# A selective-scan stage with a mixture of experts beside it: a ring of eight hidden units, second matmuls six units behind, the last gating and the expert choice moved to later steps

## The reference, cut to what matters

```python
# the scan, for 256 channels and 16 states (log/exp form in chunks of 32 tokens)
dA  = jnp.minimum(jnp.exp(delta[..., None] * A[None, None]), 1.0)
dBu = delta[..., None] * Bm[:, :, None, :] * u[..., None]
states = cum_dA * (h[:, None] + jnp.cumsum(dBuk * inv, axis=1))
yk = (states * Ck[:, :, None, :]).sum(-1)
# the experts: 1 shared + 8, hidden size 512; the best two of 8 by gate_logits
shared = jnp.einsum('th,hd->td', jax.nn.silu(x_flat @ shared_w1.T), shared_w2.T)
top_k_gates, top_k_idx = jax.lax.top_k(x_flat @ gate_w.T, 2)   # then a softmax over the two
h = jnp.einsum('td,ehd->teh', x_flat, experts_w1)
expert_out = jnp.einsum('teh,edh->ted', jax.nn.silu(h), experts_w2)
selected = jnp.einsum('ted,te->td', expert_out, gates)         # every expert for every token
```

## Time and profile before

| | us |
|---|---|
| median of 3 runs | 1534.01 (1529.97 to 1536.33) |
| the profiled execution | 1531.76 |
| its span, first to last instruction | 1530.0 |
| scan steps 0 to 63 | 52.13 to 554.84 |
| TensorE busy | 1300.1 (85%) |
| VectorE busy | 1209.3 (79%) |
| ScalarE busy | 1058.9 (69%) |
| GpSimd busy | 670.4 (44%) |

### The profile page before, as it was taken

One profiled execution on the slowest core, in us unless ns is written; L12 is line 12 of the kernel. 1 busy time (PEld: TensorE's weight loads), 2 busy tenths in 40 slices (PEclk: granted clock), 3 DMA queues, 4 the chain that ended last, 5 costly groups with the idle time before them and its releaser, 6 DMA issues.

```text
span 1530.0 us, 22554 instructions
## 1 busy us (share of the span) xinstructions
PE 1300.1 (85%) x8408; PEld 504.1 (33%) x8408; DVE 1209.3 (79%) x1443; ACT 1058.9 (69%) x1839; POOL 670.4 (44%) x650
## 2 busy tenths in 40 slices
PE   4364779888976988886499999999999998999998
PEld 1111234333443443332122222222222222236963
DVE  0799988898989871765699999999999997933522
ACT  3552388668836835453179998999899986997643
POOL 0688878967978856661403112111111123111430
PEclk9675689989988998997689999999999998999999
DMA  7222222212322302421212101100010000010210
GB/s 219 66 84 69 75 85 83 89 57 83 96 69 80 88 21 55 88 48 31 43 33 50 30 30 48 23 2 2 2 23 2 2 2 19 5 30 12 74 32 28
DMA packets 63696, 75.71 MB, mean 49 GB/s; under 512 B 8633, under 2 KB 39226, under 8 KB 63458
## 3 DMA queue, kind: packets, MB, share of 16 engines
q1 hardware_dynamic: 62818, 72.70, 17.5%
q0 software_dynamic: 768, 1.57, 0.3%
HBM read 66.04 MB, written 8.21 MB: 49 GB/s over the span
## 4 chain that ended last, share of the span: by engine, by line
PE 48%; DVE 27%; issue 10%; POOL 7%; ACT 6%; DMA 1%; SPq 1%; another core or an unknown queue 0%; DVEq 0%; POOLq 0%; ACTq 0%
DVE mx L1669 16%; PE PS L974 11%; PE PS L962 6%; PE PS L730 5%; PE PS L739 5%; PE PS L931 4%; DVE D L1457 2%; POOL D L1922 2%; PE PS L1046 2%; PE PS L1061 2%; DVE PS L1443 2%; PE PS L686 2%; PE PS L1082 2%; PE PS L1070 2%; POOL D L1938 1%
## 5 line engine op out<-in xcount | busy, mean ns | idle before, releaser
L1337 ACT ACTIVATE aa<-PS 128x512 f32<-128x512 f32 x1024 | 551.7, 597 | 62.4 <-PE PS L962 51.8
L1669 DVE TENSOR_REDUCE mx<-PS 128x2 f32<-128x1024 f32 x480 | 552.5, 1216 | 16.6 <-PE PS L931 7.0
L974 PE MATMUL PS<-aa,D 128*32 128x256 f32 x4096 | 322.7, 393 | 1.5 <-ACT aa L1337 0.6
L962 PE MATMUL PS<-D 54*128 54x512 bf16 x1024 | 213.2, 391 | 13.7 <-ACT aa L1337 8.3
L2040 POOL CAST n<-nm 4x512 bf16<-4x512 f32 x15 | 9.1, 604 | 454.2 <-ACT nm L1319 454.2
L931 PE MATMUL PS<-D 51*128 51x512 bf16 x960 | 191.3, 387 | 17.7 <-DVE mx L1669 17.2
L1443 DVE TENSOR_TENSOR_SCAN PS<-PS,D 128x512 f32<-128x512 f32 x128 | 157.5, 1231 | 11.1 <-POOL D L1938 3.5
L739 PE MATMUL PS<-xnT,f_w 128*128 128x512 f32 x288 | 157.3, 640 | 5.5 <-ACT HB L1227 4.8
L1227 ACT ACTIVATE HB<-PS 128x512 f32<-128x512 f32 x144 | 84.1, 595 | 103.1 <-PE PS L739 96.1
L730 PE MATMUL PS<-HB,f_w 128*128 128x512 f32 x288 | 145.2, 614 | 5.9 <-DVE GO L1536 5.9
L974 PEld LDWEIGHTS PS<-aa,D 128*32 128x32 f32 x4096 | 84.3, 108 | 192.8 <-issue 153.9
(11 more groups left out here) (330 smaller groups left out, 1698.2 us busy)
## 6 DMA issues: line engine op xcount, KB each, us to landing
D<-bc SPq DMA_DIRECT2D x128, 256.0 KB, 3.5
GB<-gd SPq DMA_DIRECT2D x32, 256.0 KB, 3.8
D<-sc SPq DMA_DIRECT2D x72, 64.0 KB
aa<-in_L_ffn_W SPq DMA_DIRECT2D x9, 256.0 KB, 3.0
D<-in_L_ffn_W SPq DMA_DIRECT2D x9, 256.0 KB, 3.7
f_w<-in_L_ffn_experts_w SPq DMA_DIRECT2D x1, 2048.0 KB, 9.3
f_w<-in_L_ffn_experts_w SPq DMA_DIRECT2D x8, 256.0 KB, 6.0
aa<-gh SPq DMA_DIRECT2D x1, 2048.0 KB, 9.1
```

Of the source, the lines that this page charges most:

```text
L962: e.matmul(take_exp(s + hh), KS[64 * hh:64 * hh + 54, p, 128 * kb:128 * kb + 128], QP[64 * hh:64 * hh + 54, qc % 2, p, :], start=True, sto ...
L974: t = e.matmul(PS[32 * j:32 * j + 32, 7, cs], va[:, kb, 9 * h:9 * h + 32], Pt[K % 3][:, 512 * j + 256 * n:512 * j + 256 * n + 256], start= ...
L1337: e.activation(Pt[K % 3][:, c:c + 512], bank((s + hh) % 3), ACT.Exp).then_inc(S("e_free"), 1)
L1669: e.tensor_reduce(mx4[:, G % 2, b, 2 * pair:2 * pair + 2, c:c + 1], max_banks(m), AX.X, ALU.max).then_inc(freed(m)[0], 1)
```

## The change

The ring HB gets eight buffers for six. In chunks 0 to 2 `down` runs six units behind `up` where it ran four behind (the first four `down` in slots 7 to 9 where they were in 6 and 7); gatings and their additions come two slots later (slots 14, 18, ... 34 and 37 for slots 12, 16, ... 32 and 36), the last gating in slot 40 for 38, two slots after its matmuls where it was one. `gates` begins one slot later for the choices, the weights, the transposes and the row's DMA, while the Exp stays in slot 5. The copy of expert 0 (L1231) moves from slot 7 to 10, the transposes of FO from slot 39 to 41 and the addition to x_tok from 40 to 42. To make room, gT0 lies in GO[0], Am in w_al, and vv1 in `starts`, with waits for their last readers (`ffn_sum`, `starts`). Chunk 3 keeps its order.

```diff
 def late(tc):
-    return 2 if tc < 3 else 0
+    return 3 if tc < 3 else 0
...
-            gates=lambda tc: idle(GATES + 2 * late(tc) - late(tc) // 2),
-            ffn=lambda tc: idle(FFN), later=lambda tc: idle(NORM), combine=lambda: idle(COMBINE), start=nothing,
+            gates=lambda tc: idle(GATES + late(tc) + 1),
+            ffn=lambda tc: idle(FFN + 2 if tc < 3 else FFN), later=lambda tc: idle(NORM), combine=lambda: idle(COMBINE), start=nothing,
...
-            HB1 = [sa(f"HB{i}", [128, C])[:, :] for i in range(6)]
-            gT0 = sa("gT0", [8, C])
+            HB1 = [sa(f"HB{i}", [128, C])[:, :] for i in range(8)]
...
+            gT0 = GO[0][0:8, :]
...
@@ TensorE @@
             def gates(tc):
-                yield from idle(3 + 2 * late(tc) - late(tc) // 2)
+                yield from idle(7 if tc < 3 else 3)
                 w.wait_ge(S("gt"), 18 * tc + 18)
...
@@ TensorE, ffn @@
-                    elif n < 8:
-                        for u in {6: (0, 1), 7: (2, 3)}.get(n, ()):
-                            down(36 * tc + u)
-                    else:
-                        if n % 4 == 1:
-                            down(i - 5)
-                        if n % 4:
-                            down(i - 4)
+                    elif n >= 7:
+                        if n % 4 == 3:
+                            down(i - 7)
+                        if n % 4 != 2:
+                            down(i - 6)
                     yield
...
                 else:
-                    yield
+                    down(36 * tc + 30)
+                    down(36 * tc + 31)
+                    yield from idle(2)
                     for u in range(32, 36):
                         down(36 * tc + u)
-                    yield
+                    yield from idle(2)
                 yield
...
@@ ScalarE @@
             def gates(tc):
-                yield from idle(2 + 2 * late(tc) - late(tc) // 2)
+                yield from idle(5 if tc < 3 else 2)
                 w.wait_ge(S("gt"), 18 * tc + 12)
                 e.activation(mx[:, 2, :], mx[:, 2, :], ACT.Exp).then_inc(S("g_exp"), 1)
-                yield from idle(1)
+                yield from idle(2 if tc < 3 else 1)
                 w.wait_ge(S("mm_gT"), tc + 1)
                 w.wait_ge(S("d_gd"), 16 * tc)
+                w.wait_ge(S("ffn_sum"), 8 * tc)
...
-                    w.wait_ge(S("mm_down"), i - 5)
-                    e.activation(HB1[i % 6], bank(4 + i % 2), ACT.Silu).then_inc(S("hid"), 1)
-                    if n == 7:
+                    w.wait_ge(S("mm_down"), i - 7)
+                    e.activation(HB1[i % 8], bank(4 + i % 2), ACT.Silu).then_inc(S("hid"), 1)
+                    if n == (10 if tc < 3 else 7):
...
@@ VectorE, gates @@
-                yield from idle(2 + late(tc) // 2)
+                yield from idle(3 if tc < 3 else 2)
                 w.wait_ge(S("g_exp"), tc + 1)
...
@@ VectorE, ffn; the additions on GpSimd alike @@
             def ffn(tc):
-                later_by = 0 if tc == 3 else 2
+                later_by = 0 if tc == 3 else 4
                 for n in range(36):
-                    if n % 4 == (2 + later_by) % 4 and n >= 10 + later_by:
+                    if n % 4 == 2 and n >= 10 + later_by:
                         gate_expert(tc, (n - later_by) // 4 - 1)
                     yield
+                yield
                 if tc < 3:
                     gate_expert(tc, 7)
-                    yield
-                yield
+                    yield from idle(3)
                 gate_expert(tc, 8)
...
@@ SyncE's queue @@
             def gates(tc):
-                yield from idle(4 + 2 * late(tc) - late(tc) // 2)
+                yield from idle(8 if tc < 3 else 4)
```

More of the change, by code:

```diff
@@ L460, in build @@
             w_out = sa("w_out", [128, 2, 128])
-            Am = sa("Am", [128, 32])
+            Am = w_al[:, :, :].rearrange("p g n -> p (g n)")
             f_w1 = sa("f_w1", [128, 9, 512])
@@ L493, in build @@
             pp2, yy2, vv2 = (pp_, GO[0]), (yy, GO[1]), (vv[:, :], FO[:, :])
-            ey, vp = (yy, pp_), (vv[:, :], sa("vv1", [128, C])[:, :])
+            ey, vp = (yy, pp_), (vv[:, :], starts[:, :])
             xn2 = sa("xn2", [128, 4, 128])
@@ L729, in down @@
                     w.wait_ge(S("g_row"), tc + 1)
-                e.matmul(down_bank(tc, n // 4), f_w2[:, n // 4, n % 4, :], HB1[i % 6], start=(n % 4 == 0),
+                e.matmul(down_bank(tc, n // 4), f_w2[:, n // 4, n % 4, :], HB1[i % 8], start=(n % 4 == 0),
                          stop=(n % 4 == 3)).then_inc(S("mm_down"), 1)
@@ L1172, in prolog @@
                     w.wait_ge(S("p_dl"), 2 * tc)
+                    w.wait_ge(S("starts"), 1)
                     e.activation(vp[g], bank(7), ACT.Relu, bias=w_db[:, g:g + 1]).then_inc(S("p_vv"), 1)
```

## The result

The changed kernel takes 1540.32 us (median of 6 runs, 1537.25 to 1541.47), the kernel before 1530.26 beside it (6 runs, 1528.16 to 1536.33). The ratio is 1.0046, 95% interval 1.0031 to 1.0061. The two medians stand 10 us apart; by the ratio it is some 7 us, as it is between the profiled executions, whose spans are 1537.3 and 1530.0 us. I had forecast 1524.9 and a range of 1511 to 1535.

The account below looks back on a forecast made before the run. VectorE and TensorE were taken as nearly level, VectorE waiting some 34 us in all. Chunk gains of 3.4 and 6.3 less 0.6 made 9.1 us: 1522.7 against the profiled execution, 1524.9 as a median, range 1511 to 1535.

Parts of the forecast that it names:

- The choice one step later: VectorE, chunks 0 and 1: the logits' wait goes, an Exp wait of 1 to 2 us stays, step 23 begins 2.1 earlier.
- G is ready when it was: Chunks 0 and 1: the Exp's end still sets the weights' start, so the transposes of G stay at 218.63 in chunk 0.
- rival C: Transposes of G come late in every chunk, later than 219.8 in chunk 0: 11.5 us lost, time 1545; chance 0.10.
- The row's DMA at nothing: SyncE's queue: gate rows land 3 us later, but the gating needing them is 4 to 5 us later; no cost.
- From the transposes to the first gating: TensorE, chunks 0 and 1: one more `up` there, +0.6 us; gating 1 waits 2.6 us; gain so far 2.8 us.
- The last gating: Chunk 0's end: gating 8's 3.57 us wait goes, TensorE idles 1 us for 2.35, four `down` take 3.70; gain 3.4 us.
- The new wait of L1557: Addition to x_tok waiting for the transposes of FO: about 2.6 us in chunk 0, nothing in chunk 1.
- Chunk 2: G comes 2.1 us later, TensorE 1.2 us behind, addition to x_tok at 569.5 for 568.91: loss 0.6 us, bounds 0 and 2.1.
- The sum by chunks: Chunk 0 gains 3.4 us, chunk 1 gains 6.3, chunk 2 loses 0.6: together 9.1 us.
- A: TensorE isn't at its floor and keeps up, so all gatings' waits go: 28 us gained, time 1506; chance 0.16.
- B: Waits are handed on: four `down` and convolution at the lower clock, chunk 2 loses 2.1; gain 1.4, time 1532.6; chance 0.22.

Follow-up runs that it names:

- e1: The changed kernel with one input of each of the choice's three small products in PSUM, one reduction a chunk added: 1532.00 us, 0.9988 of the kernel before.
- e2: The changed kernel with choice, Exp, weights, transposes of G and row of gates in their old slots: 1532.48 us, 0.9989 of the kernel before.
- e3: As e1, with the addition to x_tok behind the product y*z in chunks 0 to 2: 1526.08 us, 0.9950 of the kernel before.
- e6: The changed kernel with only the addition to x_tok moved behind the product y*z in chunks 0 to 2: 1526.43 us, 1.0011 of the kernel before.
- e8: As e2, with the addition to x_tok moved behind the product y*z: 1517.50 us, 0.9939 of the kernel before.
- e9: As e8, with GpSimd's product ahead of its addition of expert 8, addition to x_tok another slot later: 1524.20 us, 0.9992 of the kernel before.
- e5: The kernel before with nine added 128x4 VectorE instructions behind the first scanP of steps 3 to 11: 1528.83 us, one run.
- e4: The kernel before with nine added 128x4 VectorE instructions right behind the second scanX of steps 3 to 11: 1528.25 us, one run.

## Why the prediction was wrong, step by step

- **The choice one step later, 2.1 us in chunks 0 and 1.** This is the step that failed. The sum held the moved instructions at their old durations and never asked what GpSimd does beside their new places: "I cost this at nothing" was written for the DMA, but for the small products nothing was written at all. They measured 1.24 and 1.97 us more a chunk, 9.6 us in three. Step 23 began at 221.40 for 220.60, where I had 2.1 earlier. (0.66 us of every time after the change is a later start: step 16 began at 163.11 for 162.45.)
- **The same term was no gain by the prediction's own numbers.** It lets gating 1 wait 2.6 us for TensorE. A VectorE that came 2.1 us later would have waited 0.5 and been done at the same moment. The 2.8 us came from the later place of the gating; "of it 2.1 from the choice" was wrong, and that e1 is no faster than e2 agrees with this. In e1, with short products, step 23 didn't even come earlier: 58.25 us behind step 16, before 58.15, since VectorE then waited 1.6 us for ScalarE's squares. In e3 it came 56.19 us behind, as forecast, so this differs between executions.
- **G is ready when it was.** Wrong by 2.9 us, 0.66 of it the later start: 221.53 for 218.63. Its own working missed that the arrival of VectorE, not the Exp, would end last there; L1521 at 218.50 waited for nothing. Before, VectorE arrived at 217.54 - 1.86 = 215.68. Less the logits' wait of 0.97 us (202.30, VectorE before), plus the 2.1 of mulW and scanX, that is 216.8, only 0.7 us ahead of the Exp's end and not 1 to 2; the 1.24 us of the first longer instruction alone are more. The point that I had set for rival C, 219.8, was passed. C had the place right and the cause wrong: it let Exp or weights slip by a mulW and a scanX, and put nearly half of its price on more slow passes, which didn't come. Its 1545 us is the nearest of my figures by luck.
- **The row's DMA at nothing.** Right: no gating waited for the gate rows.
- **From the transposes to the first gating.** Right: 240.19 - 221.53 = 18.66 us, before 236.62 - 218.63 = 17.99, forecast 0.6 more. The gating waited 2.8, 2.4 and 4.4 us (forecast 2.6, as much, near 5).
- **The last gating.** Right in the mechanism: no wait of gating 8 in chunks 0 and 1, TensorE's pause 1.10 us for 2.35, the four `down` in 3.70 us for 5.40 at a clock of 1.00, the convolution behind them at 3.70 again.
- **The new wait of L1557.** Forecast 2.6 us in chunk 0, none in chunk 1, no more than 0.6 lost in chunk 2; measured 3.16, 0.69 and 2.98. In chunk 1 another wait that I hadn't looked for came before it, 2.1 us of L1573 for ScalarE: "the wait goes and nothing replaces it" was wrong there.
- **Chunk 2.** The loss of 0.6 was mis-sized: it measured 4.0. From step 50 (446.39) to the transposes of G it took 46.25 us, before 484.62 - 444.82 = 39.80: 6.45 more, of which I had 2.1. The two longer products are 3.2 of it and y*z of this chunk, 1.3 more.
- **The sum by chunks.** Chunk 0, from step 16 to step 34, gained 0.7 us (forecast 3.4); chunk 1, to step 50, lost 1.6 (forecast a gain of 6.3); chunk 2, to its last addition, lost 4.0 (forecast 0.6). 0.7 us were lost before step 16 and 1.8 behind the last addition: 7.3 between the two spans.
- **Two rivals.** A falls: gatings 1 still wait and TensorE went pass after pass, 18.20 busy of 18.20 us. B was right in kind for the choice (e1 against e2), wrong in its reason: not slow passes, but a TensorE that is no earlier.

Put together, by ratios: ring and later gatings -0.11% (e2), the later choice +0.57% on top of it, of which the longer products are all, within 0.2% (e1). The waits for FO that the later gatings brought are some 0.35 to 0.5% more that they could have had (e6, e8). e2's own -0.11% can't be told from zero, so the gatings' gain was eaten almost whole. By the rows that was done by the waits that they caused (6.8 us at L1557, 3.8 at L1573 in e2) and by the 3.3 us of y*z, which is as long in e2 as in the change. For the waits at L1557 e6 and e8 show it; for y*z no run does, since e9, which shortens it, makes other waits longer.

## What to carry to other kernels

When an instruction is moved, look not only at what it waits for but at who is running beside it in its new place. VectorE and GpSimd stop each other by operand: a 0.16 us instruction moved behind the scan that releases GpSimd took up to 2.13 us, and 0.16 again once one input lay in PSUM. When waits fall and the kernel doesn't, compare busy time at equal instruction counts and list it by line and shape.

## What the runs showed of the hardware

- Beside GpSimd's TENSOR_TENSOR of 128x1024 the stop lasts to its end and goes by the operands, not by the size: 128x4 with both inputs in SBUF, or one input SBUF to SBUF in TENSOR_SCALAR, ended with GpSimd's product (1.20 and 1.21 us in e5), with one input in PSUM 0.15 us.
- Beside GpSimd's TENSOR_SCALAR of 128x512 the stop of a difference of two SBUF inputs was shorter or absent: 0.61 us when begun 0.09 us into it, 0.17 when begun 0.54 us into it, both done 0.86 us before it.
- It works both ways. In e8 GpSimd's product beside y*z took 2.89 us for 2.35 (306.34), and its small copy beside y*z before the change 0.69 for 0.19 (311.09).
- 0.15 us decide. Started that much ahead of GpSimd's product (e4) the same instruction took 0.14 to 0.20 us.
